# Second edge layer of a graph network: additions, type masks and score sums moved between engines

## The reference

```python
Q = (enh @ Wq + bq); K = (enh @ Wk + bk); V = (enh @ Wv + bv)      # each (N, 4, 64)
rel = rel_w[edge_relations]                                         # (E, 64), 64 types
mod_k = K[src] + 0.2 * rel[:, None, :]
scores = einsum('ehd,ehd->eh', Q[dst], mod_k) / 64 ** 0.5
seg_max = segment_max(scores, dst); ex = exp(scores - seg_max[dst])
w = ex / segment_sum(ex, dst)[dst]
agg = segment_sum(w[:, :, None] * V[src], dst)
```

## Time and profile before

| | us |
|---|---|
| median of 3 timed runs | 1843.47 |
| lowest and highest of them | 1840.63, 1845.88 |
| the profiled execution, its own time | 1847.34 |
| its span in the profile | 1845.6 |

### The profile page before, as it was taken

The page is one execution under the profiler, slowest core; times in us unless marked ns, Lnnn a source line. Parts: engine busy times, 40 slices in busy tenths (PEclk is TensorE's granted clock), DMA queues, the critical chain, the costliest instruction groups (busy, mean ns, idle before and its releaser), DMA issues. The chain is left out here.

```text
span 1845.6 us, 29221 instructions
## 1 busy us (share of the span) xinstructions
PE 1307.0 (71%) x7043; PEld 921.3 (50%) x7043; DVE 1403.1 (76%) x3587; ACT 935.2 (51%) x3225; POOL 1085.2 (59%) x1146
## 2 busy tenths in 40 slices
PE   6346656665566468999795787877787878867086
PEld 5234434443344366777453455555555555456075
DVE  6558888888889962544867899999999999675444
ACT  3345555545545352332351476777777777346043
POOL 3677777777777200000416777777777777474556
PEclk9668777777777758999997799999999999876588
DMA  5566666667666209200247888888888888436392
GB/s 151 157 186 209 206 215 204 206 208 208 214 205 198 85 1 321 81 1 1 91 171 254 261 262 259 250 267 264 273 263 271 253 270 255 136 114 154 142 333 65
DMA packets 168854, 353.60 MB, mean 192 GB/s; under 512 B 27831, under 2 KB 64776, under 8 KB 168564
## 3 DMA queue, kind: packets, MB, share of 16 engines
q0 software_dynamic: 58192, 175.85, 31.4%
q1 hardware_dynamic: 106501, 172.46, 28.7%
q10 hardware_dynamic: 4000, 3.41, 0.6%
HBM read 268.43 MB, written 87.33 MB: 193 GB/s over the span
## 5 line engine op out<-in xcount | busy, mean ns | idle before, releaser
L827 POOL DMA_INDIRECT e_rows<-h_rows,src_col x416 | 414.8, 997 | 136.8 <-issue 123.4
L1345 POOL DMA_INDIRECT e_rows<-kv_rows,src_col x320 | 307.0, 959 | 101.2 <-issue 67.3
L1104 PE MATMUL e_sum<-e_rows,e_of_dst 128*128 128x264 f32 x832 | 294.5, 497 | 85.6 <-DVE e_rows L926 78.3
L1564 ACT ACTIVATE e_rows<-e_rows 128x64 f32<-128x64 f32 x1152 | 281.4, 336 | 0.3
L1627 PE MATMUL e_query<-q,e_to_dst 128*128 x1248 | 203.6, 295 | 75.1 <-DVE e_rows L1398 56.9
L1104 PEld LDWEIGHTS e_sum<-e_rows,e_of_dst 128*128 128x128 f32 x832 | 177.7, 240 | 126.1 <-DVE e_rows L926 82.2
L1667 PE MATMUL e_sum<-e_rows,e_of_dst 128*128 128x260 f32 x640 | 187.4, 416 | 1.3 <-POOL e_rows L1274 0.7
L1627 PEld LDWEIGHTS e_query<-q,e_to_dst 128*128 128x128 bf16 x1248 | 120.2, 100 | 131.4 <-issue 92.0
L1029 ACT ACTIVATE e_rows<-e_rows 128x32 f32<-128x32 f32 x832 | 181.0, 305 | 0.1
L1486 DVE TENSOR_TENSOR acc<-acc,e_sum 128x260 f32 x346 | 145.5, 420 | 42.1 <-DVE acc L1486 19.4
L1345 POOL DMA_INDIRECT x<-kv_rows,src_col x96 | 91.7, 955 | 73.4 <-POOLq L2149 39.8
(11 more groups left out here) (429 smaller groups left out, 2728.5 us busy)
## 6 DMA issues: line engine op xcount, KB each, us to landing
step_of<-e_of_dst SPq DMA_DIRECT2D x104, 256.0 KB, 2.2
e_of_dst<-step_of SPq DMA_DIRECT2D x104, 256.0 KB
sorted_rows<-zeros SPq DMA_DIRECT2D x1, 14560.0 KB
comb<-sorted_rows SPq DMA_DIRECT2D x56, 260.0 KB
e_rel<-step_rel SPq DMA_DIRECT2D x26, 512.0 KB, 4.3
step_to<-e_to_dst SPq DMA_DIRECT2D x26, 512.0 KB, 5.7
e_to_dst<-step_to SPq DMA_DIRECT2D x52, 256.0 KB
e_rows<-h_rows,src_col POOLq DMA_INDIRECT x416, 3.3
```

The source lines that it names most:

```text
L827: pool.indirect_dma_start(out=g[t // BATCH % R][:, t % BATCH, :], out_offset=None, in_=k.h_rows[:, :], in_offset=bass.IndirectOffsetOnAxis ...
L1104: pe.matmul(psm[t % NB], of_dst[q][:, s % GROUP, :], g[m % R][:, s, :], start=True, stop=True).then_inc(summed, 1)
L1345: pool.indirect_dma_start(out=rows_at(t, 1)[:, 0, :], out_offset=None, in_=k.kv_rows[:, :], in_offset=bass.IndirectOffsetOnAxis(ap=k.src_c ...
L1564: ins = act.activation(x, x, ACT.Copy, scale=row[:, plo + h:plo + h + 1])
```

## The change

- All 416 additions are made by VectorE. `by_pool`, `take` and GpSimd's additions are gone; GpSimd only gathers (and makes messages in the last steps, as before). TensorE waits for the addition of step t - 3 in every case.
- The type masks are made ahead, in `feed_first`: SP loads the labels in 26 parts into a ring of three tiles, GpSimd compares each with the type number, and SP stores the result to a new DRAM tensor `step_same`. The second edge layer loads finished masks, in one DMA instead of two per two chunks.
- The score sums of pairs 5, 8 and 11 of every lot are made by ScalarE: for each of 2 steps and 4 heads one copy of 64 columns in place, with an accumulator output. They come after the messages of steps 6, 13 and 20 of the lot at hand; for lot 0 before the first probabilities.

```diff
@@ allocate
+    k.labels_in = [ctx.enter_context(nc.semaphore(f"labels_in{b}")) for b in range(3)]
+    k.masks_kept = [ctx.enter_context(nc.semaphore(f"masks_kept{b}")) for b in range(2)]
+    k.step_same = dram("step_same", [P, STEPS // 2 * P], BF16)
@@ edges_second
-    by_pool = [t for t in range(TAIL) if t % BATCH in (3, 7, 13)]
+    ACT_PAIRS = {5: 6, 8: 13, 11: 20}
...
-            for half in two:
-                steps = slice((h + half) * CHUNK, (h + half + 1) * CHUNK)
-                sp.dma_start(to_typ[h // 2 % 2][half * F:(half + 1) * F, :],
-                             k.step_typ[steps, :].rearrange("s e -> (s e)").partition_broadcast(F)
-                             ).then_inc(labels_in[b], 16)
+            sp.dma_start(to_typ[h // 2 % 2][:, :], k.step_same[:, h // 2 * CHUNK * P:(h // 2 + 1) * CHUNK * P]
+                         ).then_inc(labels_in[b], 16)
...
         for t in range(STEPS - SLOTS2):
-            if t % 8 == 0:
-                w = load_windows(t, 8)
-            if t in pool_no:
-                j = pool_no[t]
-                pool.wait_ge(copied, j + 1)
-                pool.wait_ge(added, t)
-                pool.tensor_tensor(acc[:, w[t % 8], :], acc[:, w[t % 8], :], taken[j % NS][:, :], ALU.add
-                                   ).then_inc(added, 1)
             pool.wait_ge(summed, t + 1)
             gather_row(t + SLOTS2)
...
-        def masks(h):
-            v.wait_ge(*labels_of(h))
-            typ = to_typ[h // 2 % 2]
-            v.tensor_scalar(typ[:, :], typ[:, :], typ_no[:, 0:1], None, ALU.is_equal).then_inc(masks_ready, 1)
...
         def score_reduce(m, q):
+            if q in ACT_PAIRS:
+                return
...
         def add(t, w):
-            if t < 0 or t in pool_no:
+            if t < 0:
                 return
...
+        def score_reduce(m, q):
+            act.wait_ge(look_used, m * PAIRS2 + (q + 1))
+            keys = rows_at(m * LONG + q * QP, QP)
+            for t in range(QP):
+                for h in range(H):
+                    x = keys[:, t, h * F:(h + 1) * F]
+                    ins = act.activation(x, x, ACT.Copy, accum_out=sc2[:, q * QP + t, h:h + 1])
+            ins.then_inc(scored, 1)
+
+        for q in ACT_PAIRS:
+            score_reduce(0, q)
         for m in range(LOTS2):
             probabilities(m)
             act.wait_ge(prob_in_rows, m + 1)
             for s in range(LONG):
                 t = m * LONG + s
                 message(t)
-                if s > NB:
-                    take(t - NB)
+                for q, after in ACT_PAIRS.items():
+                    if s == after and m + 1 < LOTS2:
+                        score_reduce(m + 1, q)
...
             if q % CHUNK_PAIRS == 0:
-                pe.wait_ge(masks_ready, h // 2 + 1)
                 pe.wait_ge(*labels_of(h))
...
-            if t >= NB and t - NB in pool_no:
-                pe.wait_ge(copied, pool_no[t - NB] + 1)
-            elif t >= NB:
+            if t >= NB:
                 pe.wait_ge(added, t - NB + 1)
@@ feed_first
+        SAME, PARTS, RING = 8 * P, STEPS // 16, 3
+        labels = [sb(f"labels{b}", [P, SAME], BF16) for b in range(RING)]
...
+            def load_labels(g):
+                b = g % RING
+                if g >= RING:
+                    sp.wait_ge(k.masks_kept[(g - RING) % 2], k.kept_before[(g - RING) % 2] + 16 * ((g - RING) // 2 + 1))
+                for half in range(2):
+                    at = (2 * g + half) * 8
+                    sp.dma_start(labels[b][half * F1:(half + 1) * F1, :],
+                                 k.step_typ[at:at + 8, :].rearrange("s e -> (s e)").partition_broadcast(F1)
+                                 ).then_inc(k.labels_in[b], 16)
+
+            def keep_same(g):
+                sp.wait_ge(same_made, g + 1)
+                if g >= 2:
+                    sp.wait_ge(k.masks_kept[g % 2], k.kept_before[g % 2] + 16 * (g // 2))
+                sp.dma_start(k.step_same[:, g * SAME:(g + 1) * SAME], labels[g % RING][:, :]
+                             ).then_inc(k.masks_kept[g % 2], 16)
+
+            for g in range(PARTS + 2):
+                if g < PARTS:
+                    load_labels(g)
+                if g >= 2:
+                    keep_same(g - 2)
             sp.wait_ge(k.w_in, 16 * QKV_LOADS)
+            for j in range(2):
+                sp.wait_ge(k.masks_kept[j], k.kept_before[j] + 16 * len(range(j, PARTS, 2)))
...
+            for g in range(PARTS):
+                b = g % RING
+                pool.wait_ge(k.labels_in[b], k.labels_before[b] + 32 * (g // RING + 1))
+                pool.tensor_scalar(labels[b][:, :], labels[b][:, :], typ_no[:, 0:1], None, ALU.is_equal
+                                   ).then_inc(same_made, 1)
```

More of the change, by code:

```diff
@@ L742, in edges_first @@
     look = ps("look", [P, BANK])[:, 0:3 * PH].rearrange("p (s j h) -> p s j h", j=3, h=H)
-    steps_in = [sem(f"steps_in{b}") for b in ring]
+    steps_in = k.labels_in
     rows_in = [sem(f"rows_in{b}") for b in ring]
@@ L768, in edges_first @@
     BY_POOL = {(m, q): j * 2 + i + 1 for j, m in enumerate((LAST_BATCH - 1, LAST_BATCH)) for i, q in enumerate((1, 2))}
-    kept = [sem(f"one_hots_kept{j}") for j in two]
+    kept = k.masks_kept
     PER_BATCH = 16 * (1 + GROUPS)
+    k.labels_before = [32 * len(range(b, BATCHES, R)) for b in ring]
+    k.kept_before = [PER_BATCH * len(range(b, BATCHES, 2)) for b in two]
     bias_in, all_bias_in = k.loads_in, k.expect_loads(1)
@@ L1248, in edges_second @@
     summed = sem("summed")
-    copied = sem("copied")
     added = sem("added")
     def labels_of(h):
-        loads = sum(1 if u % 2 else 4 if u * CHUNK % LONG == 0 else 3 for u in range(h % 2, h + 1, 2))
+        loads = sum(1 if u % 2 else 3 if u * CHUNK % LONG == 0 else 2 for u in range(h % 2, h + 1, 2))
         return labels_in[h % 2], 16 * loads
@@ L1490, in _ @@
         c.inc(v.memset(acc[:, :, :], 0.0))
-        c.link(v.tensor_scalar(typ_no[:, :], k.iota_col[:, 0:1], float(F), -float(F), ALU.is_ge, ALU.mult))
-        c.link(v.tensor_tensor(typ_no[:, :], typ_no[:, :], k.iota_col[:, 0:1], ALU.add))
-        masks(0)
         for q in range(PAIRS2):
@@ L1527, in _ @@
                     made = reduce_contexts(made)
-                ahead = (m + 1) * LONG // CHUNK + q // 4 + 1
-                if q % 8 == 5 and ahead < CHUNKS:
-                    masks(ahead)
                 if more:
@@ L1573, in probabilities @@
             act.activation(prob[:, :], diff[:, :], ACT.Exp).then_inc(prob_ready, 1)
-            if m:
-                take(m * LONG - NB)
             act.wait_ge(transposed, 2 * m + 2)
@@ L1581, in probabilities @@
             ins.then_inc(prob_in_rows, 1)
-        def take(t):
-            if t not in pool_no:
-                return
-            j = pool_no[t]
-            act.wait_ge(summed, t + 1)
-            if j >= NS:
-                act.wait_ge(added, by_pool[j - NS] + 1)
-            act.copy(taken[j % NS][:, :], psm[t % NB]).then_inc(copied, 1)
+        def score_reduce(m, q):
[8 more added lines that the diff above has]
+            score_reduce(0, q)
         for m in range(LOTS2):
@@ L1986, in _ @@
             sp.wait_ge(k.w_in, 16 * QKV_LOADS)
+            for j in range(2):
+                sp.wait_ge(k.masks_kept[j], k.kept_before[j] + 16 * len(range(j, PARTS, 2)))
         @block.gpsimd
         def _(pool):
-            pool.memset(zeros[:, 0:2 * D], 0.0).then_inc(zeros_ready, 1)
-            pool.memset(zeros[:, 2 * D:COMB], EMPTY).then_inc(zeros_ready, 1)
+            pool.memset(zeros[:, 0:2 * D], 0.0).then_inc(consts_ready, 1)
+            pool.memset(zeros[:, 2 * D:COMB], EMPTY).then_inc(consts_ready, 1)
@@ new lines, in _ @@
+            pool.wait_ge(consts_ready, 2)
+            pool.iota(typ_no[0:F1, :], pattern=[[0, 1]], base=0, channel_multiplier=1,
+                      allow_small_or_imprecise_dtypes=True).then_inc(consts_ready, 1)
+            pool.wait_ge(consts_ready, 3)
+            pool.iota(typ_no[F1:P, :], pattern=[[0, 1]], base=0, channel_multiplier=1,
+                      allow_small_or_imprecise_dtypes=True).then_inc(consts_ready, 1)
+            pool.wait_ge(consts_ready, 4)
+            for g in range(PARTS):
[3 more added lines that the diff above has]
+                                   ).then_inc(same_made, 1)
```

22 lines of the change are left out of this document (4 added, 18 removed).

## The result

| | us |
|---|---|
| before, median of 4 timed runs | 1843.87 (1840.63 to 1845.88) |
| after, median of 4 timed runs | 1861.39 (1859.39 to 1864.28) |
| ratio, 95% interval | 1.010 (1.0085 to 1.0114) |
| the profiled execution after, and its span | 1861.75, 1860.0 |

The change makes the kernel 17.5 us slower. The forecast was 9.5 us slower, 1853.0, in a range from 1840 to 1866: the direction and the range hold, the size is off by 8.4 us.

The account below looks back on a forecast made before the run. VectorE was taken to bound the second edge layer's middle stretch: +44.1 - 11.2 - 10.2 - 6.3 - 6.5 = +9.9 us. With -0.4 in the opening, +9.5 on the median 1843.47 gave 1853.0 us, range 1840 to 1866.

Parts of the forecast that it names:

- Rest ... Nothing: Second layer's mask loads move the same 256 KB per two chunks and the tail keeps its work: no cost.
- The middle stretch: Second edge layer, 1041 to 1578 us, bound by VectorE: all terms there sum to +9.9 us.
- 36 reductions leave (gross): Middle stretch, VectorE: 36 score reductions go to ScalarE, 0.60 us each, saving 21.6 us before any wait.
- Additions: Middle stretch, VectorE: 70 additions from GpSimd turn lone additions into pairs, 0.63 us each, +44.1 us.
- The completion wait: Slots 6, 9, 12: the multiplication waits for the relation addition; 0.29 us of each reduction returns as idleness, leaving -11.2 us.
- the completion wait is free: Rival, slots 6, 9, 12: no wait between relation addition and multiplication, total -0.9, 1842.6 us; chance 0.22.
- Other waits: Middle stretch, VectorE: 6.3 us of waits for GpSimd go, and 6.5 of 9.2 for factor, rows and sums.
- Masks on VectorE: Middle stretch: 22 mask instructions leave VectorE at 0.465 us each, -10.2 us.
- ScalarE as the bound: Rival: from 0.51 us a sum, a lot's third sum delays TensorE's turn of the scores, 1860 to 1880 us; chance 0.14.
- The masks fit the first experts: GpSimd's 26 masks, 2.6 us each, every 3.8 us, done near 850 us, hidden up to 5.0 us a mask.
- a sign of being wrong: A second edge layer starting later than 977 us was listed among observations that would show the forecast wrong.
- The opening: Second layer, 977 to 1041 us: an earlier start is given back to the gathers; only one mask counts, -0.4 us.

Follow-up runs that it names:

- the two groups of kernels: Eight kernels with GpSimd's additions kept and no comparisons on it, experts at 697.3 us in the mean; eleven with the comparisons, 705.6: 8.3 us.
- seven profiles before: Profiles of seven kernels with the second layer as before the change; lots of 546.9 to 552.0 us, 549.7 in the mean.
- four after: Four profiles with the change's own second layer; lots of 557.5, 560.5, 558.7 and 563.1 us, 560.0 in the mean.
- the transfers alone: The kernel before plus only SP's label loads and stores to step_same, no mask made, nothing reading it; 1842.08 us, ratio 0.9989.

## Why the prediction was too low

**The first edge layer is the step that failed.** The text ended the change's list with "Rest ... Nothing", and never asked what the first layer's pace hangs on. It is 8.1 us of the 14.4 between the two profiles and 8.3 us between the two groups of kernels, about all that the forecast lacks. The profile before would have shown that GpSimd's gathers run there without a pause (416 in 540.2 us), so that what lengthens GpSimd's work there lengthens the layer (after, its gathers are busy 8.2 us longer and the experts start 8.1 us later), and that 66 of them take over 1.0 us. That instructions 150 us later touch it, no view of before could tell.

**The middle stretch came out as forecast, by two errors that cancel.** Forecast: +9.9. The first pair of profiles says +5.5 over the lots, but lots of the same code differ by 5 us from profile to profile; seven profiles before (549.7) and four after (560.0) say +10.3. The ledger of VectorE's pitches over the lots, mean of the same profiles, beside the forecast's terms:

| term | forecast, us | measured, us |
|---|---|---|
| 70 additions become pairs | +44.1 | +45.5 |
| 36 reductions leave (gross) | -21.6 | -22.1 |
| wait between relation addition and multiplication | +10.4 | +4.2 |
| masks leave | -10.2 | -11.1 |
| waits for GpSimd, factor, rows, sums | -12.8 | -6.2 (what is left of 10.3) |

- *Additions*: right, 0.64 us a pair.
- *The completion wait*: mis-sized. It costs 0.12 us (0.71 to 0.72 in all 36 slots, for 0.60), not the 0.29 taken from the pair of additions. The rival "the completion wait is free" was nearer in its place, 6.2 us better than charged, but it did not give its 1842.6. The trace shows 0.12 us for this pair and 0.29 for the additions (0.63 for 0.34), so this pair lies between the two bounds of the forecast, nearer to the free wait. Why the additions pay more isn't shown.
- *Other waits*: over-credited by 6.6 us. The forecast counted all 6.3 us of waits for GpSimd and 6.5 of the other 9.2 as won. Over the lots, in the mean of the same profiles, the waits for GpSimd fall from 7.7 us to nothing and those for rows from 3.1 to 1.0, but the waits for TensorE's sums and the factor rise from 4.7 to 7.8. Besides, the rescaling starts 0.83 us after the multiplication of a freed slot (1239.72, 1240.55), where 0.59 to 0.60 stand in the slots beside it.
- *Masks on VectorE*: right. By themselves they were worth 3.8 us of the lots and the sums 0.3 (one profile each), since GpSimd's 44.9 us stand right behind the 46.0 of a lot. The text saw that row and dismissed it by the 6.3 us of waits that it then caused; for the whole change, which takes the additions off GpSimd, that did no harm.

**ScalarE does not become the bound.** A sum takes 0.24 us where I took 0.35 and set the point of decision at 0.51. The rival with this mechanism, ScalarE as the bound, is out.

**The masks fit the first experts.** They take 2.84 us each against 2.6, and are done at 866 where I said 850 and the limit was 880. The 1 us of issue in a mask's 3.8 us was my guess, from no row; a mask comes every 4.13 us (759.0 to 862.3, 25 pitches). The second layer does start later than 977 us, at 987.8, which the text named as a sign of being wrong; but the cause was ahead of the experts, not in them.

**The opening**: right. TensorE's first look-up waits 8.3 us for a load where it waited 13.10 us for the first mask, and the time from first gather to first e_diff is 56.0 us as before.

## What to carry to other kernels

Before costing an edit at nothing outside its stage, list the stages that an engine paces without a pause: here 7 ns on each of 416 gathers, with starts some 15 ns nearer to VectorE's, went with 8.3 us in the first layer, where the masks alone brought 3.8 us in the lots. When one engine is relieved, look at once at the one whose own sum per turn lies 1 us below: two parts that spare VectorE 11 us or more were worth 0.3 and 3.8 us of the lots alone. And take a step of a few microseconds from several profiles: the same lots differed by 5 us between profiles.

## What was not expected of the hardware

GpSimd's indirect gathers of the first layer take 942/946 ns (least/median) in the program before, 949/953 with 26 comparisons of a 128x1024 tile with a column later in the program, and 952/957 when the 70 additions with register addresses are taken out of it; 28 more memsets, other semaphores, another DRAM order, the transfers alone or longer programs of the other engines leave the 942. Why later instructions lengthen an earlier gather stays open; the second layer's gathers don't show it (940/946 before and after). A gather that starts under VectorE's comparison of 128x512 elements, with more than 0.15 us of it left, ends 0.81 to 0.83 us after it where it is held (39 of 41 before, 48 of 48 after); of those that start more than 0.21 us ahead of it, 1 of 60 before and 0 of 45 after take over 1.0 us. A comparison of 128x1024 bf16 elements with a column takes GpSimd 2.84 us and VectorE 0.48 to 0.55.
